# A six-layer decoder on one core: PSUM banks paired freely, the context transposed ahead of the kernel, and a new instruction order

## The chip, the cores and the metric

The kernel runs on one core of one Trainium2 chip. The metric is the device time of one execution in microseconds (us), as the median of several runs. TensorE is called PE, VectorE DVE, ScalarE ACT, GpSimd POOL and SyncE, which issues all transfers here, SP.

## The reference

Sixteen entries of 256 tokens by 256 features pass six layers, each followed by a residual sum and a layer norm without weights. `ctx_1024` is a second input of 16 x 256 x 256. Everything is float32.

```python
x = _layernorm(x + _L0_attn_ref(x, ...))                     # linear attention over 16 heads per token, then an MLP of 1024
x = _layernorm(x + _L0_xattn_ref(x, ctx_1024, ctx_1024, ...))  # 16 heads, softmax over keys at most 64 tokens away
x = _layernorm(x + _L0_ffn_ref(x, ...))                      # six cells, each 8-head softmax attention over three earlier nodes
x = _layernorm(x + _L1_attn_ref(x, ...))                     # causal linear attention, 16 heads
x = _layernorm(x + _L1_xattn_ref(x, ctx_1024, mask, ...))    # 16 heads, softmax over all 256 keys, mask on the keys
x = _layernorm(x + _L1_ffn_ref(x, ...))                      # fft, one matrix in the frequency domain, ifft: one 256 x 256 product
```

In both cross attentions the context goes through key and value projections: `k = key @ Wk.T + bk`, `v = value @ Wv.T + bv`.

## The kernel before, in words

**Data.** An entry is held as ten slots of 128 x 512 floats in `work` (four entries at a time, `NS = 4`), as tokens by features or, for a matmul's contraction, as features by tokens. Weights stay in `weights`, or pass through a ring of four slots that SP refills (`stream`). The eight PSUM banks (2 KB per partition each, 128 x 512 floats) are declared as four tensors `banks0` to `banks3` of two banks each.

**Order.** The program is a list of steps: `setup_steps` folds weights once, `entry_steps` names an entry's steps. A step has an engine, a name, a duration for the planner, the steps that it needs and the banks that it takes. `program_plan` walks through time with these durations, and whenever an engine is idle it starts the waiting step of the earliest entry, among them the one with the longest `tail` (the path behind it, times a drawn factor between 1 and 1.3). The result, `PLAN`, is for each engine a fixed list of steps; five functions (`tensor`, `vector`, `scalar`, `gpsimd`, `sync`) turn it into instructions and semaphore waits. So each engine runs its list in order, and a step that waits holds up all behind it on its engine.

**Banks.** `pick` chooses banks: a step of kind `score` or `kept` takes a whole tensor (banks 2u and 2u+1), a step of kind `misc` or `ctx` one bank, among banks 4 to 7 or beside one already taken. `take` makes PE wait for the eviction of what the bank held before. A semaphore `s_evicted` exists for each pair (0 to 3) and for each bank used alone (4 to 11, bank b is 4 + b).

**Softmax attention** (`heads`, 20 times per entry, four or eight heads' worth each): `s` multiplies queries by keys into two pairs (line L872), DVE takes the maxima of each pair (L1233), `nm` transposes them on PE into one bank (L883), ACT copies them (L1450), `st` multiplies again, transposed and less the maximum, into two pairs (L897 and L901; with L729 for the band mask), ACT takes the exponential of each pair into SBUF (L1466), `pv` multiplies by the values (L925, and L932 for the row sums in the cells) into the bank that `kept` left over.

**Other steps the text names.** `transposes` (L707) turns an entry's 256 x 256 block by four PE transposes into one bank, and ACT or DVE evicts it. `ctx_t` does so with the context when an entry is loaded (slot RAW into slot CT, for `x_k` and `x_v`), `ctx_t2` again before `y_k`, from a second load (`again`, L1727, into slot AGAIN), as CT is reused by the cells. `a_qkv` projects the first layer's queries, keys and values; its eviction (L1189) adds biases that lie in `row`, which SP loads in one transfer (L1706). `mix1` and `mix2` are that layer's products on POOL (L1614, L1624) and sums on DVE (L1199, L1203), 16 pieces per entry.

## Time and profile before

| | |
|---|---|
| median of 3 runs | 3605.32 us (3601.53 to 3610.42) |
| the profiled execution: its span (first to last instruction) | 3599.7 us |
| PE busy | 3245.1 us (90% of the span) |
| DVE busy | 2282.5 us (63%) |
| ACT busy | 1713.9 us (48%) |
| POOL busy | 1019.3 us (28%) |
| mean granted clock of PE | 0.974 |

The profiled execution was taken apart from the three timed runs, and only its span is known; the median lies 5.6 us above the span. Busy time is the time in which an engine had at least one instruction in work. Each float32 matmul of the code stands as two records in the profile, a transpose as one.

### The profile page before, as it was taken

The numbers are of one execution on the slowest core, as the hardware profiler recorded it, in microseconds if no ns is written. First come the engines' busy times: TensorE is split into PE (matmuls) and PEld (weight loads), VectorE is DVE, ScalarE is ACT, GpSimd is POOL, SyncE is SP. The second block draws the span as 40 slices with busy tenths as digits, with TensorE's granted clock in tenths as the row PEclk, the third lists the DMA queues.
The fourth block names the chain that finished last, engine by engine and source line by source line (L and its number), as shares of the span: only waits on it lengthen the run. The fifth ranks groups of instructions, "written<-read, shape, count | busy, mean of one in ns | idle before, by whom it ended". The sixth has DMA issues, their size and how long they took to land.

```text
span 3599.7 us, 77605 instructions
## 1 busy us (share of the span) xinstructions
PE 3245.1 (90%) x31500; PEld 2402.1 (67%) x31500; DVE 2282.5 (63%) x4093; ACT 1713.9 (48%) x3466; POOL 1019.3 (28%) x795
## 2 busy tenths in 40 slices
PE   7899989999989989999999999999999999998876
PEld 6777666666676667766666776666677666766654
DVE  6665757647766766667676666767667576465633
ACT  1245454544545454554545555454555545554532
POOL 7942305103242504214060421506042150000000
PEclk9899999999999999999999999999999999999987
DMA  6211010100011101011010101101010110000000
GB/s 213 71 45 39 22 42 16 31 31 22 23 51 31 36 13 49 25 35 35 17 45 16 48 25 31 36 19 45 16 48 25 31 35 15 31 16 13 13 7 4
DMA packets 123132, 122.88 MB, mean 34 GB/s; under 512 B 9760, under 2 KB 122656, under 8 KB 122656
## 3 DMA queue, kind: packets, MB, share of 16 engines
q1 hardware_dynamic: 122784, 117.91, 10.9%
q8 instruction: 258, 4.23, 0.5%
q14 instruction: 90, 0.74, 0.1%
HBM read 113.69 MB, written 4.19 MB: 33 GB/s over the span
## 4 chain that ended last, share of the span: by engine, by line
PE 61%; DVE 13%; POOL 9%; ACT 8%; issue 7%; DMA 1%; SPq 0%; DVEq 0%; POOLq 0%; ACTq 0%
PE banks L722 16%; PE banks L714 13%; PE banks L897 7%; PE banks L925 6%; PE banks L872 6%; DVE nmx L1233 5%; POOL work L1614 5%; ACT work L1466 4%; POOL work L1624 3%; PE banks L707 2%; PE banks L883 2%; PE banks L729 2%; PE banks L932 2%; PE banks L901 1%; PE banks L1004 1%
## 5 line engine op out<-in xcount | busy, mean ns | idle before, releaser
L722 PE MATMUL banks<-work,weights 128*128 128x256 f32 x3584 | 861.9, 388 | 40.5 <-DVE work L1256 22.1
L1233 DVE TENSOR_REDUCE nmx<-banks 128x4 f32<-128x1024 f32 (+1 forms) x640 | 720.9, 1165 | 251.5 <-PE banks L872 249.1
L722 PEld LDWEIGHTS banks<-work,weights 128*128 128x128 f32 x3584 | 671.3, 192 | 177.1 <-issue 55.2
L1466 ACT ACTIVATE work<-banks 128x1024 f32<-128x1024 f32 (+1 forms) x640 | 596.5, 980 | 268.7 <-PE banks L901 266.9
L714 PE MATMUL banks<-weights,work 128*128 128x256 f32 x2688 | 661.0, 392 | 44.0 <-ACT work L1466 16.6
L714 PEld LDWEIGHTS banks<-weights,work 128*128 128x128 f32 x2688 | 505.0, 195 | 147.3 <-issue 47.7
L1624 POOL TENSOR_TENSOR work<-work 128x512 f32<-128x512 f32 x256 | 405.5, 1609 | 212.3 <-DVE work L1203 115.7
L897 PE MATMUL banks<-work 32*128 32x256 f32 (+1 forms) x5120 | 396.2, 396 | 46.2 <-issue 15.6
L872 PE MATMUL banks<-work 32*128 32x256 f32 (+1 forms) x5120 | 355.0, 393 | 36.2 <-issue 11.0
L1250 DVE TENSOR_TENSOR added<-work 128x1024 f32<-128x1024 f32 x192 | 261.5, 1363 | 171.7 <-ACT work L1466 164.1
L925 PE MATMUL banks<-work 128*32 128x256 f32 (+3 forms) x5632 | 334.6, 359 | 23.7 <-ACT work L1466 23.6
L1614 POOL TENSOR_TENSOR work<-work 128x512 f32<-128x512 f32 x256 | 341.0, 1358 | 49.8 <-DVE work L1199 32.2
L1658 POOL TENSOR_TENSOR work<-work,row 128x512 f32<-128x512 f32 x64 | 88.8, 1387 | 882.1 <-PE banks L707 882.1
L897 PEld LDWEIGHTS banks<-work 32*128 32x128 f32 x5120 | 213.3, 189 | 165.8 <-issue 97.3
L872 PEld LDWEIGHTS banks<-work 32*128 32x128 f32 x5120 | 234.9, 187 | 128.9 <-issue 108.3
L1365 ACT ACTIVATE work<-banks,cb 128x256 f32<-128x256 f32 x384 | 161.4, 473 | 251.7 <-PE banks L722 251.6
L925 PEld LDWEIGHTS banks<-work 128*32 128x32 f32 x5632 | 156.6, 110 | 163.8 <-issue 102.4
L1203 DVE TENSOR_REDUCE work<-work 128x32 f32<-128x512 f32 x256 | 173.1, 679 | 90.8 <-POOL work L1624 90.6
L1199 DVE TENSOR_REDUCE work<-work 128x32 f32<-128x512 f32 x256 | 172.2, 680 | 75.2 <-POOL work L1614 75.0
L1450 ACT ACTIVATE work<-banks 128x256 f32<-128x256 f32 x320 | 118.7, 385 | 189.7 <-PE banks L883 189.1
L707 PE MATMUL banks<-ident,work 128*128 128x128 f32 x896 | 140.1, 286 | 68.8 <-DVE work L1181 28.3
L901 PE MATMUL banks<-work,ones_bf 3*128 3x256 bf16 (+1 forms) x2560 | 191.4, 272 | 0.0
(157 smaller groups left out, 3518.3 us busy)
## 6 DMA issues: line engine op xcount, KB each, us to landing
weights<-in_w_all SPq DMA_DIRECT2D x322, 256.0 KB, 2.7
work<-in_w_setup SPq DMA_DIRECT2D x41, 256.0 KB, 5.5
work<-in_ctx SPq DMA_DIRECT2D x32, 256.0 KB, 2.9
work<-in_x SPq DMA_DIRECT2D x16, 256.0 KB, 3.0
out<-work SPq DMA_DIRECT2D x16, 256.0 KB, 2.2
weights<-in_w_all SPq DMA_DIRECT2D x1, 3072.0 KB, 16.9
row<-in_rows SPq DMA_DIRECT2D x1, 1664.0 KB, 10.1
mrow<-in_mask SPq DMA_DIRECT2D x16, 32.0 KB, 3.1
```

What stands on the lines that cost most here:

```text
L707: ins = e.transpose(b[:, f * 256 + c * P:f * 256 + c * P + P], src[:, c, f * P:f * P + P], ident[:, :])
L714: ins = e.matmul(b[:, m * 256:m * 256 + 256], xin[:, k, m * P:m * P + P], wslot(w)[:, k, :], start=(k == 0 and (m == 0 or closed)) if star ...
L722: ins = e.matmul(b[:, m * 256:m * 256 + 256], wslot(w)[:, k, m * P:m * P + P], xin[:, k, :], start=(k == 0 and (m == 0 or closed)) if star ...
L872: ins = e.matmul(b[g // 2][:, g % 2, cc * 256:cc * 256 + kk.stop - kk.start], q[32 * g:32 * g + 32, f, cc * P:cc * P + P], k[32 * g:32 * g ...
L897: e.matmul(b[g // 2][:, g % 2, o], k[32 * g:32 * g + 32, f, kc * P:kc * P + P], q[32 * g:32 * g + 32, f, qq], start=(kind != "x"), stop=False,
L901: ins = e.matmul(b[g // 2][:, g % 2, o], ones_bf[32 * g:32 * g + 3, :], upper(stored_nmax(s, a))[32 * g:32 * g + 3, qq], start=False, stop ...
L925: ins = e.matmul(b[32 * g:32 * g + 32, lo:hi], left, right[:, kc * 256 + lo - qq.start:kc * 256 + hi - qq.start], start=(kc == 0), stop=(k ...
L1233: e.tensor_reduce(nmax(s, n)[:, 2 * p:2 * p + 2, :], b, AX, ALU.max, negate=True).then_inc(*freed("max", n, p, i))
L1250: e.tensor_tensor(added[:, half], pt(half, 0, 4)[:, :, 0:S], pt(half, 0, 4)[:, :, S:2 * S], ALU.add).then_inc(*tell(vec[s], "added", a, i))
L1466: e.activation(dst, src, ACT.Exp).then_inc(*freed("exp", n, p, i))
L1614: e.tensor_tensor(big1, q.unsqueeze(2).broadcast_to([P, PH, NH, DH]), k.unsqueeze(1).broadcast_to([P, PH, NH, DH]), ALU.mult).then_inc(*te ...
L1624: e.tensor_tensor(big2, mix.unsqueeze(2).broadcast_to([P, PH, DH, NH]), v.unsqueeze(1).broadcast_to([P, PH, DH, NH]), ALU.mult).then_inc(* ...
```

## The change: what it does

1. **Banks.** One tensor `banks` holds all eight. A `score` or `kept` step may take any two free banks; it prefers neighbours. If they are not neighbours, the eviction (the maxima on DVE, the exponentials on ACT) is two instructions of half the size. A single bank may be any free one. One semaphore per bank; a pair uses that of its first bank.
2. **Context.** The host passes `ctx_1024` with its last two axes exchanged. It is loaded straight into slot CT. The steps `ctx_t` and `ctx_t2` and their evictions are gone; `again` waits for `ck` of cell 5 (the last reader of CT's content) where it waited for `cv` of cell 5.
3. **Order.** `tail` is multiplied by ten drawn factors (one up to 1.3, nine up to 1.08, from other seeds). The planner adds 0.2 us (ACT) or 0.06 us (DVE) for a split eviction.
4. **Biases.** The first three rows of `row`, those of `a_qkv`, are loaded on their own, between entry 0's x and its context; the rest after entry 1's x.

```diff
-BANKS, PAIRS, HALVES, LONG = 8, 4, 2, 2
-SINGLE = range(4, BANKS)
+BANKS, HALVES, LONG = 8, 2, 2
...
-    ctx_t = through("ctx_t", 0, 0.44, "ACT", 0.49, load)
...
-            again = do("SP", "again", 0, 2.6, cv[c])
-            ctx_t2 = through("ctx_t2", 0, 0.44, "ACT", 0.48, again, ck[c])
-            y_k = through("y_k", 0, 1.75, "DVE", 0.66, ctx_t2, ("DVE", "centre", "y_k"))
+            again = do("SP", "again", 0, 2.6, ("PE", "ck", c))
+            y_k = through("y_k", 0, 1.75, "DVE", 0.66, again, ("DVE", "centre", "y_k"), also=(("PE", "co", c - 1),))
...
-    tail = [t * (1 + 0.3 * v) for t, v in zip(tail, rng.random(len(steps)))]
+    for n, seed in enumerate(SEEDS):
+        spread = 0.08 if n else 0.3
+        tail = [t * (1 + spread * v) for t, v in zip(tail, np.random.default_rng(seed).random(len(steps)))]
...
-                found = [u for u in range(PAIRS) if bank_left[2 * u] and bank_left[2 * u + 1]]
-                if found:
-                    bank_left[2 * found[0]] = bank_left[2 * found[0] + 1] = False
+                found = sorted(((u, v) for u in range(BANKS) for v in range(u + 1, BANKS) if bank_left[u] and bank_left[v]),
+                               key=lambda u: (u[1] - u[0] > 1, neighbours(bank_left, u[0]) + neighbours(bank_left, u[1]), u))
+                for u in found[:1]:
+                    bank_left[u[0]] = bank_left[u[1]] = False
...
-                found = sorted((u for u in range(BANKS) if bank_left[u] and (u in SINGLE or not bank_left[u ^ 1])), key=lambda u: (bank_left[u ^ 1], -u))
+                found = sorted((u for u in range(BANKS) if bank_left[u]), key=lambda u: (neighbours(bank_left, u), -u))
...
+                if apart(e, i, n):
+                    us += 0.2 if e == "ACT" else 0.06
...
-        pair = [ctx.enter_context(nc.psum_tensor(f"banks{u}", [P, 2, 512], F32)) for u in range(PAIRS)]
-        unit = pair + [pair[b // 2][:, b % 2, :] for b in range(BANKS)]
+        banks = ctx.enter_context(nc.psum_tensor("banks", [P, BANKS, 512], F32))
...
-        evicted = [signal(f"s_evicted{u}") for u in range(len(unit))]
+        evicted = [signal(f"s_evicted{u}") for u in range(BANKS)]
...
+        def spans(*key):
+
+            u = home.get(key, (0, 1))
+            if u[1] == u[0] + 1:
+                return [(0, 2, banks[:, u[0]:u[0] + 2, :])]
+            return [(j, j + 1, banks[:, u[j]:u[j] + 1, :]) for j in range(2)]
...
-                    once("rows")
-                    if a == 0:
-                        e.wait_ge(*when("ctx_t mm", i))
+                    once("first rows")
...
+                    for j, end, b in spans("max", n, p, i):
+                        ins = e.tensor_reduce(nmax(s, n)[:, 2 * p + j:2 * p + end, :],
+                                              b.rearrange("p j (c n) -> p j c n", c=NC)[:, :, :, 0:w], AX, ALU.max, negate=True)
+                    ins.then_inc(*freed("max", n, p, i))
...
+                    for j, end, b in spans("exp", n, p, i):
+                        dst = pt(half_of.get((i, n), 0), 2 * p + j, end - j).rearrange("p j (c n) -> p j c n", c=NC)[:, :, :, 0:w]
+                        ins = e.activation(dst, b.rearrange("p j (c n) -> p j c n", c=NC)[:, :, :, 0:w], ACT.Exp)
+                    ins.then_inc(*freed("exp", n, p, i))
...
-                    e.dma_start(slot(s, RAW), of_entry(ctx_in, i)).then_inc(*tell(in_ctx[s], "ctx", i))
+                    if i == 0:
+                        e.dma_start(row[:, 0:FIRST_ROWS, :].rearrange("p r n -> p (r n)"),
+                                    rows[0:FIRST_ROWS * D].partition_broadcast(P)).then_inc(*tell(in_first_rows, "first rows"))
...
+                    e.dma_start(slot(s, CT), of_entry(ctx_in, i)).then_inc(*tell(in_ctx[s], "ctx", i))
...
-                    e.wait_ge(*when("cv mm", 5, i))
-                    e.dma_start(slot(s, AGAIN), of_entry(ctx_in, i)).then_inc(*tell(in_ctx[s], "ctx again", i))
+                    e.wait_ge(*when("ck mm", 5, i))
+                    e.dma_start(slot(s, CT), of_entry(ctx_in, i)).then_inc(*tell(in_ctx[s], "ctx again", i))
...
-        "x": a["x"], "ctx": a["ctx_1024"], "mask": a["mask_BxS2_bk0"],
+        "x": a["x"], "ctx": a["ctx_1024"].transpose(0, 2, 1), "mask": a["mask_BxS2_bk0"],
```

The table of the order shows what this moves. The first place is the start of the program on PE. The names: `work` holds the entries' slots, `ident` is the identity, `s_loaded_ctx0` counts transfers of the context into entry slot 0, `s_vector0` steps of DVE on that slot (here layer norm 1). Before:

```order
L707 MATMUL banks3<-ident,work 128x128 [waits s_loaded_ctx0,s_setup_vector,s_setup_gpsimd]
L707 MATMUL banks3<-ident,work 128x128 x3
L707 MATMUL banks3<-ident,work 128x128 [waits s_evicted11,s_loaded_ctx1]
L707 MATMUL banks3<-ident,work 128x128 x3
L707 MATMUL banks3<-ident,work 128x128 [waits s_vector0]
L707 MATMUL banks3<-ident,work 128x128 x3
L714 MATMUL banks3<-weights,work 128x256 [waits s_evicted11,s_streamed_weights0,s_evicted10]
```

Now (L732 is the line of the transposes, L739 that of the projections):

```order
L732 MATMUL banks<-ident,work 128x128 [waits s_vector0,s_setup_vector,s_setup_gpsimd]
L732 MATMUL banks<-ident,work 128x128 x3
L739 MATMUL banks<-weights,work 128x256 [waits s_evicted7,s_streamed_weights0]
L739 MATMUL banks<-weights,work 128x256 x3
L732 MATMUL banks<-ident,work 128x128 [waits s_vector1]
```

The two groups of transposes of the context ahead of entry 0's first projection are gone. Over the whole program PE has 896 transposes on this line before and 768 now, ACT 112 copies of such blocks (128x512) before and 80 now.

The second place is the middle of the program on PE, where entry 7 (its maxima are in `nmx3`) goes through the last attention. `s_vector3` stands for DVE's maxima being ready; `s_evicted2` is the semaphore of pair 2, that is of `banks2`, and `s_evicted9` that of bank 5, its second half. Before:

```order
L901 MATMUL banks1<-work,ones_bf 128x256 x2
L901 MATMUL banks2<-work,ones_bf 128x256 x2
L883 MATMUL banks2<-ident,nmx3 128x128 [waits s_evicted2,s_vector3]
L883 MATMUL banks2<-ident,nmx3 128x128
L872 MATMUL banks0<-work 128x256 [waits s_evicted0,s_evicted3,s_evicted9]
L872 MATMUL banks0<-work 128x256
L872 MATMUL banks3<-work 128x256 x2
L872 MATMUL banks0<-work 128x256 x2
L872 MATMUL banks3<-work 128x256 x2
L883 MATMUL banks2<-ident,nmx3 128x128 [waits s_evicted9,s_vector3]
```

Now (L917 and L921 are the lines of `st`, L903 that of `nm`, L945 that of `pv`; `s_evicted0` is the semaphore of bank 0 and of the pair of banks 0 and 1):

```order
L917 MATMUL banks<-work 128x256 [waits s_evicted4,s_evicted1,s_evicted0]
L917 MATMUL banks<-work 128x256 x3
L921 MATMUL banks<-work,ones_bf 128x256 x4
L917 MATMUL banks<-work 128x256 x4
L921 MATMUL banks<-work,ones_bf 128x256 x4
L917 MATMUL banks<-work 128x256 [waits s_evicted7,s_evicted6,s_evicted2]
L917 MATMUL banks<-work 128x256 x3
L921 MATMUL banks<-work,ones_bf 128x256 x4
L917 MATMUL banks<-work 128x256 x4
L921 MATMUL banks<-work,ones_bf 128x256 x4
L903 MATMUL banks<-ident,nmx3 128x128 [waits s_evicted0,s_vector3]
```

Before, the transposes of the maxima take a bank of `banks2` straight behind the group that wrote `banks2`. Now a second whole `st` group stands between the group that wrote banks 0 and 1 and the transposes that take one of them.

Counted over the program, DVE takes 640 maxima of pairs before, and now 596 of pairs and 88 of single banks; ACT 640 exponentials of pairs before, and now 601 of pairs and 78 of single banks. So 44 pairs are split on DVE and 39 on ACT. PE changes between its three tile forms (full, 32 rows, 32 columns) 1453 times before and 1435 times now.

## Rows read from the trace of the kernel before

**Rows 1.** The page: busy time, share and instructions of each engine.

```profile
PE 3245.1 (90%) x31500; PEld 2402.1 (67%) x31500; DVE 2282.5 (63%) x4093; ACT 1713.9 (48%) x3466; POOL 1019.3 (28%) x795
```

**Rows 2.** Busy time of the engines in stretches (start, seven periods, end).

```profile
0.00:200.00 200.00, 163.75 (x968) 135.87 (x969) 133.05 (x259) 48.60 (x97) 166.67 (x148) 0.91 0.43 137
1395.70:1606.90 211.20, 196.37 (x1946) 145.19 (x1945) 140.66 (x253) 106.53 (x217) 63.96 (x48) 0.98 0.11 31
...
2660.75:2871.40 210.65, 195.45 (x1948) 144.62 (x1948) 141.44 (x253) 106.91 (x218) 63.32 (x48) 0.99 0.11 31
3400.00:3599.70 199.70, 137.49 (x1226) 95.98 (x1218) 78.81 (x152) 69.02 (x138) 6.48 (x7) 0.82 0.02 6
```

**Rows 3.** Timeline, SP: stores of entries 3, 12 and 15.

```profile
1145.36 0.38 SPq L1730 DMA_DIRECT2D out<-work  x1
...
3048.91 0.38 SPq L1730 DMA_DIRECT2D out<-work  x1
...
3597.03 0.38 SPq L1730 DMA_DIRECT2D out<-work  x1
```

**Rows 4.** Who PE waited for in 1806 to 2017 us (one period).

```profile
PE banks L722 <- DVE work L1256: 2.0, 1, 2.0
PE banks L925 <- ACT work L1466: 1.7, 2, 1.2
PE banks L897 <- issue: 1.6, 1, 1.6
...
PE banks L883 <- ACT work L1466: 1.2, 1, 1.2
```

**Rows 5.** Timeline, PE, 1963 to 1971 us.

```profile
1963.96 0.29 PE L901 MATMUL banks<-work,ones_bf 3*128 3x256 bf16 x4
1965.49 0.41 PE L883 MATMUL banks<-ident,nmx 128*128 128x128 f32 x2 [1.24 <-ACT work L1466]
...
1970.77 0.71 PE L897 MATMUL banks<-work 32*128 32x256 f32 x8 [0.73 <-ACT work L1466]
```

**Rows 6.** Timeline, ACT, same stretch.

```profile
1964.32 1.94 ACT L1466 ACTIVATE work<-banks 128x1024 f32<-128x1024 f32 x2 [1.50 <-PE banks L901]
```

**Rows 7.** Timeline, PE, 1861 to 1877 us.

```profile
1861.13 1.99 PE L722 MATMUL banks<-work,weights 128*128 128x256 f32 x8 [2.04 <-DVE work L1256]
...
1876.90 1.15 PE L897 MATMUL banks<-work 32*128 32x256 f32 x8 [1.60 <-issue]
```

**Rows 8.** Groups by line and shape (busy us, mean ns).

```profile
L1233 DVE TENSOR_REDUCE nmx<-banks 128x4 f32<-128x1024 f32 x512 | 603.8, 1218 | 232.6 <-PE banks L872 231.3
L1466 ACT ACTIVATE work<-banks 128x1024 f32<-128x1024 f32 x512 | 499.5, 1023 | 213.0 <-PE banks L901 212.5
L707 PE MATMUL banks<-ident,work 128*128 128x128 f32 x896 | 140.1, 286 | 68.8 <-DVE work L1181 28.3 <-DVE ykb L1089 10.2 <-ACT work L1466 7.4
L1203 DVE TENSOR_REDUCE work<-work 128x32 f32<-128x512 f32 x256 | 173.1, 679 | 90.8 <-POOL work L1624 90.6
L1310 DVE TENSOR_TENSOR work<-banks,causal 128x512 f32<-128x512 f32 x128 | 79.1, 680 | 13.2 <-PE banks L1004 13.1
L1393 ACT ACTIVATE work<-banks 128x512 f32<-128x512 f32 x112 | 66.1, 597 | 80.8 <-PE banks L707 80.6
```

**Rows 9.** Timeline of the start.

```profile
11.40 1.28 ACT L1393 ACT_TABLE_LOAD   x1 [11.40 <-PE banks L707]
...
13.68 0.56 SPq L1706 DMA_DIRECT2D row<-in_rows  x1
14.60 0.29 ACT L1371 ACTIVATE lnv<-mv,eps 128x2 f32<-128x2 f32 x1
...
18.18 3.78 PE L714 MATMUL banks<-weights,work 128*128 128x256 f32 x8 [1.11 <-ACT work L1365]
...
23.84 0.69 DVE L1189 TENSOR_TENSOR work<-banks,row 128x512 f32<-128x512 f32 x1 [4.52 <-issue]
```

**Rows 10.** Line L1727 (`again`): its transfers.

```profile
DMA to landing us min/median/max: 2.6/2.7/2.8
```

More of the change, by code:

```diff
@@ L200, in entry_steps @@
     x_t = through("x_t", 0, 0.44, "ACT", 0.48, x)
-    x_k = through("x_k", 0, 1.75, "ACT", 1.8, ctx_t, ("PE", "z2_t", 0))
+    x_k = through("x_k", 0, 1.75, "ACT", 1.8, ("PE", "z2_t", 0))
     x_v = through("x_v", 0, 1.75, "ACT", 0.56, clear)
@@ L340, in program_plan, with neighbours, apart @@
     bank, half, long_held = [True] * BANKS, [True] * HALVES, [0]
+    def neighbours(left, u):
+        return (u > 0 and left[u - 1]) + (u + 1 < BANKS and left[u + 1])
+    def apart(e, i, n):
+        return e != "PE" and any(j != "rest" and isinstance(held[i, m][j][1], tuple) and held[i, m][j][1][1] - held[i, m][j][1][0] > 1
+                                 for m, j in freed_by[n])
     def pick(takes):
@@ L794, in tensor @@
                     product(take("misc", "four", a), FOURIER[a][1]).then_inc(*tell(setup_pe, "four mm", a))
-                elif op == "ctx_t":
-                    e.wait_ge(*when("ctx", i))
-                    transposes(take("misc", "ctx_t", i), slot(s, RAW)).then_inc(*tell(pe[s], "ctx_t mm", i))
-                elif op == "ctx_t2":
-                    e.wait_ge(*when("ctx again", i))
-                    transposes(take("misc", "ctx_t2", i), slot(s, AGAIN)).then_inc(*tell(pe[s], "ctx_t2 mm", i))
                 elif op == "z_t":
@@ L1704, in sync @@
                         operand(f"{n}{a}", in_node[a], "node operands", a)
-                    if a == 2:
-                        e.dma_start(row[:, :, :].rearrange("p r n -> p (r n)"), rows.partition_broadcast(P)).then_inc(
-                            *tell(in_rows, "rows"))
                 elif op == "fourier":
```

96 lines of the change are left out of this document (48 added, 48 removed).

## The prediction

> **What bounds the kernel now.** I read the page's busy times first: PE works 3245 us of 3599.7, the next engine, DVE, 2283 [rows 1]. So PE is the bound, and 355 us are its idle time. The windows show where that lies [rows 2]: 36 us in the first 200, 62 in the last 200, and in between a repeating pattern. In seven periods, one for each entry, of 210.5 to 211.2 us, PE is busy 194.9 to 196.4 and idle about 15.3 (210.8 less 195.5), while DVE works 141 and ACT 106. The stores say how far the pattern carries: entry 3 is stored at 1145 us, entry 12 at 3049, nine periods of 211.5; the three entries behind it end at 3597 [rows 3]. A gain can come from less work on PE, or from smaller gaps in it.
>
> What the gaps are is in the waits of one period [rows 4]: one of 2.0 us behind DVE's weighing of a head pair (L1256), then many of 0.4 to 1.6 us behind the exponentials (L1466) and some that the profile puts down to nothing ("issue"). One of them can be read exactly. At 1965.49 us PE waits 1.24 us to transpose maxima [rows 5]. In the order of before, these transposes take a bank of `banks2` straight behind the `st` group that filled `banks2`, so they stand until both exponentials, 1.94 us from 1964.32, are done [rows 6]. PE's work was ready; a bank was not.
>
> **The change, part by part.** Against the profiled execution's 3599.7 us:
>
> *Transposes of the context.* PE loses 128 of 896 transposes. They take 140.1 us / 896 = 0.156 us each [rows 8], so 20 us. Bounds: 10, if half of them stood in gaps that stay; 30, with their share of the idle time before this line, 68.8 / 896 x 128 = 10. ACT loses 32 copies of 0.6 us [rows 8], nothing on a half-idle engine. Value: -20.
>
> *Gaps in the middle.* The new order decides here. For every bank that PE takes, and every result that it needs, I added the durations of the matmul groups between the group that the eviction follows and the one that waits, and compared that with what the evicting instructions take (1.22 us for a pair's maxima, 1.02 for its exponentials [rows 8], the rest from their own groups). Where the matmuls are the shorter, the difference is a shortage. This is an estimate: it knows no queueing on DVE and ACT. It gives 9.4 us of shortage per entry before, for entries 3 to 12, against 15.3 measured, and 7.6 of the 9.4 are banks. It finds the wait above as 1.2 us. In the new order it gives 3.6. The difference, 5.8 us, times 10 entries is 58; scaled by 15.3 / 9.4 it is 94; and if a third of the removed shortages come back as queueing, 40. I take 60, near the unscaled end, as the part that the count doesn't explain may stay. Value: -60.
>
> *The first three entries and the start.* The same count gives 16.9 us per entry before and 9.3 now, 23 in all. At the start itself, ACT loads a table for the context's copy (at 11.40), and then a second one, so that layer norm 1 goes on at 14.60 [rows 9]. Without the copy one load of 1.28 us and the copy are gone from this path, about 2 us. The first projection ends near 22 (18.18 + 3.78), and DVE evicts it only at 23.84, when the biases are there (issued at 13.68 [rows 9]): their own early transfer gives 1.9 us more. Up to 27 in all; but the first 200 us also hold 167 us of POOL work [rows 2], which nothing here shortens, so 4 is the lower bound. Value: -20.
>
> *The end.* The last three entries have 29.7 us of shortage each before and 28.9 now: no gain. PE's idle 62 us at the end are one entry's own chain. Value: 0.
>
> *Split evictions.* On DVE 44 pairs are two instructions. A half-size one is nearest to the 128x512 read of banks of 0.680 us, so a split costs 2 x 0.680 - 1.218 = 0.14 us, 6 us in all; on ACT 2 x 0.597 - 1.023 = 0.17, times 39 is 7 [rows 8]. DVE has 70 idle us in a period and ACT 104; PE waits for a split only where a bank is short. Between 0 and 13. Value: +3. If the cover is gone, it is the full 13.
>
> *The second load of the context* now lands where `y_k` reads it, with no transpose between. It takes 2.7 us to land [rows 10]; between `ck` of cell 5 and `y_k` the new order has two attention groups and a projection, 4.5 us of matmuls. It stays hidden, and the weight loads behind it on SP with it. Should it be late, PE loses at most the 2.7 us per entry, 43 us. `x_v` waits for the first load, which is there half an entry before. Value: 0.
>
> *PE's clock.* The granted clock is 0.98 to 0.99 in the periods [rows 2]: a stretch of each runs at 1.2 instead of 2.4 GHz. It follows the largest gaps: after waits of 2.04 and 1.60 us the group of eight at 1876.90 takes 1.15 us, where its like takes 0.71 [rows 5, 7]. A mean of 0.985 over 211 us is 6 us at the low level, so 3 us lost. The new order has no shortage above 1.0 us in a period. Between 0 and 3 us per period, 0 to 36 over twelve; as the clock may fall for other gaps too, I take 8. Value: -8.
>
> The Trainium skill has a rule on this (TensorE: Matmul & The Clock Gate, "A second HAM failure mode: psum-queue depth-cycling"): small idle times between groups that cycle through PSUM banks can make the clock swing between its two levels and cost throughput. By that rule the clock's whole loss belongs to the gaps that go, and the term would be 36; the row allows it and doesn't prove it, so 8 stands.
>
> Sum: 20 + 60 + 20 + 8 - 3 = 105, so a span of 3495. The median of before lies 5.6 us above the span of its profile, and 3605.3 - 105 = **3500 us**. With all low ends (10 + 40 + 4 + 0 - 13 = 41, 3564) and most of the high ends (30 + 94 + 27 + 0 = 151, 3454) its own range is 3454 to 3564.
>
> **The rivals.**
>
> *The clock recovers too (12%).* As forecast, but the clock term is its upper bound: 28 us more, 3472. For it: the low clock follows the largest gaps. Against it: the mean of 0.98 to 0.99 is already near 1.
>
> *Banks were not what PE waited for (13%).* The gaps move: where PE found no bank it now finds DVE or ACT still at other work, since each engine runs a fixed list. Then only transposes and the start count: 20 + 4 - 3 = 21, 3584. For it: the largest wait of a period (L1256) and 6 of the 15 us are not in my count. Against it: the wait at 1965.49 is a bank's, and DVE is 67% busy.
>
> *No change (5%).* The transposes filled gaps, and the ends set the time: 3595 to 3615. Against it: PE is 93% busy in a period.
>
> *Slower (8%).* One mechanism: the drawn priorities put `mix2` and `mix1` sums (L1203, L1199, 0.68 us each, 32 per entry [rows 8]) ahead of maxima that PE waits for. In the new order such a sum stands directly ahead of a head group's maxima 26 times in the whole program, before 17 times. Each costs PE at most 0.68 us; the forecast's 105 us are used up at 105 / 16 / 0.68 = 10 such late maxima per entry. With 20 per entry: 3500 + 16 x 20 x 0.68 = 3718; with 12, 3630. Against it: 26 is under 2 per entry.
>
> **Chances and range.** The forecast has 62%. Within 0.3% (11 us) a measurement of this kernel can't tell a change from none. Faster by more: 62 + 12 + 13 = 87%; same 5%; slower 8%. The range must leave out no more than 2 in 10. Without the second rival it would; with it, it goes to 3585. It starts at 3450, the forecast's high end, which holds the clock rival too.
>
> **What would show it.** Right: a period of about 203 us (211 less 1.3 for transposes, about 6 for gaps and up to 1 for the clock) with PE busy 194 and idle 9; entry 3 stored near 1115; waits behind L1466 and L1233 cut by half; the last entry's 62 us unchanged; DVE and ACT busy times within 2 us per period of before; no wait of `y_k` for the transfer. Wrong: a period whose idle stays near 15 with other names in the waits (the second rival), or one in which PE waits for maxima behind L1203 (the last). The most likely error is the size of the middle term, which rests on a count of distances, not on a measured wait.

## The result, and the profile after

The changed kernel takes 3567.21 us (median; 3565.31 to 3568.85) against 3603.64 of the kernel before on the same chip: ratio 0.9906, 95% interval 0.9892 to 0.9920. It is faster, by 36 us and not by 105; the forecast of 3500 us missed, though 3567 lies inside its range. The profiled execution has a span of 3566.3 us (before 3599.7) and a mean granted clock of 0.964 (before 0.974).

First the page's busy times, then the windows of the changed kernel: 200 us at either end and one of the periods between two stores.

```profile
PE 3242.3 (91%) x31372; PEld 2395.2 (67%) x31372; DVE 2329.9 (65%) x4137; ACT 1695.1 (48%) x3472; POOL 1019.1 (29%) x795
```

```profile
0.00:200.00 200.00, 166.49 (x936) 138.35 (x937) 128.04 (x247) 46.24 (x93) 164.27 (x146) 0.86 0.43 136
1323.90:1535.50 211.60, 195.70 (x1940) 143.82 (x1936) 145.64 (x255) 105.41 (x216) 63.02 (x47) 0.98 0.11 31
...
3366.30:3566.30 200.00, 138.39 (x1200) 97.02 (x1200) 78.70 (x152) 68.74 (x140) 5.78 (x7) 0.80 0.02 6
```

A period still takes 211.6 us, PE busy 195.7 and idle 15.9; before it was 210.7, 195.4 and 15.3 (means of seven periods from store 4 to store 11). Nothing was won in the middle [rows 2]. The stores (SP, timeline) of entries 3, 12 and 15 say where the 33 us of span came from.

```profile
1112.24 0.38 SPq L1750 DMA_DIRECT2D out<-work  x1
...
3016.84 0.38 SPq L1750 DMA_DIRECT2D out<-work  x1
...
3563.73 0.38 SPq L1750 DMA_DIRECT2D out<-work  x1
```

Against [rows 3], entry 3 is stored 33.2 us earlier; from there to entry 12 it is 1904.6 us (before 1903.5), and from there to the end 547 (548). All of the gain is made before entry 3 is stored.

PE's waits in one period (1747.1 to 1958.7), the answer to [rows 4]:

```profile
PE banks L747 <- DVE work L1275: 4.3, 1, 4.3
PE banks L892 <- DVE nmx L1251: 2.0, 3, 0.8
PE banks L903 <- DVE nmx L1260: 1.8, 1, 1.8
PE banks L892 <- issue: 1.6, 2, 1.3
...
PE banks L732 <- ACT work L1482: 0.4, 2, 0.2
```

The waits behind the exponentials (L1482, before L1466) are indeed nearly gone: over the whole run PE's fell from 88 to 23 us. Those behind the maxima were not cut by half, as the prediction had it, but rose from 59 to 72 (L1251, before L1233); those behind the last step of splitting the maxima rose from 16 to 36 (L1260, before L1241), behind the weighing from 33 to 55 (L1275, before L1256), behind the layer norms' last step from 28 to 48 (L1201, before L1181). The largest is one wait of 4.3 us at `co` (a cell's output projection) of cell 0 (L747), in every period. The timeline shows how it arises:

```profile
1857.55 7.08 POOL L1641 TENSOR_TENSOR work<-work 128x512 f32<-128x512 f32 x4
...
1859.79 0.61 PE L952 MATMUL banks<-added,ones 128*32 128x256 f32 x8
1860.10 0.69 DVE L1221 TENSOR_REDUCE work<-work 128x32 f32<-128x512 f32 x1 [0.23 <-POOL work L1641]
...
1862.32 2.59 DVE L1191 SCALAR_TENSOR_TENSOR work<-work,mv,row 128x256 f32<-128x256 f32 x2
...
1864.95 0.88 DVE L1197 SCALAR_TENSOR_TENSOR work<-work,rstd 128x256 f32<-128x256 f32 x2
1865.75 0.42 DVE L1275 TENSOR_TENSOR work<-banks,work 128x256 f32<-128x256 f32 x1
...
1866.31 3.75 PE L747 MATMUL banks<-work,weights 128*128 128x256 f32 x8 [4.29 <-DVE work L1275]
```

PE has the attention's values and their row sums ready at 1860.4. The weighing by these sums (L1275) stands on DVE behind a sum of the second mix of entry i+3, which waits for GpSimd, and behind layer norm 5 of the entry before, whose first step, two instructions (L1191), takes 2.59 us while GpSimd multiplies. ScalarE's inverse sums stand behind that layer norm's root in the same way. The eight matmuls behind the wait take 3.75 us, at a granted clock of 0.66 from 1866.3 to 1873.0; such a group takes 1.97 elsewhere.

### The profile page after: what moved, and what is told of

The parts are those of the page before. It is cut to its first block, busy times and chain, and to the rows that moved or that the text cites. A ratio compares the mean times of both kernels' runs of the same rounds, so it can differ in the third digit from the quotient of the medians.

```text
span 3566.3 us, 77500 instructions
## 1 busy us (share of the span) xinstructions
PE 3242.3 (91%) x31372; PEld 2395.2 (67%) x31372; DVE 2329.9 (65%) x4137; ACT 1695.1 (48%) x3472; POOL 1019.1 (29%) x795
## 4 chain that ended last, share of the span: by engine, by line
PE 60%; DVE 15%; ACT 9%; issue 8%; POOL 7%; DMA 1%; SPq 0%; DVEq 0%; POOLq 0%; ACTq 0%
PE banks L747 16%; PE banks L739 11%; PE banks L892 7%; PE banks L917 6%; DVE nmx L1251 5%; PE banks L945 5%; POOL work L1641 3%; ACT work L1482 3%; PE banks L732 2%; PE banks L754 2%; PE banks L855 2%; PE banks L903 2%; POOL work L1631 2%; PE banks L952 1%; PE banks L921 1%
## 5 line engine op out<-in xcount | busy, mean ns | idle before, releaser
L747 PE MATMUL banks<-work,weights 128*128 128x256 f32 x3584 | 868.3, 390 | 56.4 <-DVE work L1275 51.5
L1251 DVE TENSOR_REDUCE nmx<-banks 128x4 f32<-128x1024 f32 (+3 forms) x684 | 725.4, 1099 | 250.5 <-PE banks L892 248.7
L747 PEld LDWEIGHTS banks<-work,weights 128*128 128x128 f32 x3584 | 678.3, 194 | 189.0 <-DVE work L1275 53.9
L1482 ACT ACTIVATE work<-banks 128x1024 f32<-128x1024 f32 (+3 forms) x679 | 595.1, 937 | 288.7 <-PE banks L921 288.7
L739 PE MATMUL banks<-weights,work 128*128 128x256 f32 x2688 | 653.7, 389 | 20.7 <-ACT work L1482 4.4
L739 PEld LDWEIGHTS banks<-weights,work 128*128 128x128 f32 x2688 | 499.3, 193 | 124.9 <-issue 39.7
L1641 POOL TENSOR_TENSOR work<-work 128x512 f32<-128x512 f32 x256 | 407.3, 1615 | 366.4 <-DVE work L1221 216.9
L917 PE MATMUL banks<-work 32*128 32x256 f32 (+1 forms) x5120 | 391.4, 394 | 18.0 <-DVE nmx L1251 6.8
L1631 POOL TENSOR_TENSOR work<-work 128x512 f32<-128x512 f32 x256 | 346.6, 1375 | 148.7 <-DVE work L1217 134.7
L1269 DVE TENSOR_TENSOR added<-work 128x1024 f32<-128x1024 f32 x192 | 281.3, 1469 | 129.3 <-ACT work L1482 118.7
L945 PE MATMUL banks<-work 128*32 128x256 f32 (+3 forms) x5632 | 341.2, 364 | 5.3 <-ACT work L1482 4.6
L917 PEld LDWEIGHTS banks<-work 32*128 32x128 f32 x5120 | 214.0, 190 | 132.1 <-issue 81.2
L945 PEld LDWEIGHTS banks<-work 128*32 128x32 f32 x5632 | 158.3, 111 | 148.4 <-issue 82.4
L1221 DVE TENSOR_REDUCE work<-work 128x32 f32<-128x512 f32 x256 | 173.2, 678 | 86.2 <-POOL work L1641 85.7
L1466 ACT ACTIVATE work<-banks 128x256 f32<-128x256 f32 x320 | 119.2, 385 | 212.7 <-PE banks L903 212.3
L921 PE MATMUL banks<-work,ones_bf 3*128 3x256 bf16 (+1 forms) x2560 | 190.8, 272 | 0.0
L732 PE MATMUL banks<-ident,work 128*128 128x128 f32 x768 | 122.1, 285 | 67.0 <-DVE work L1201 47.6
```

Of the source, the lines that this page charges most:

```text
L732: ins = e.transpose(b[:, f * 256 + c * P:f * 256 + c * P + P], src[:, c, f * P:f * P + P], ident[:, :])
L739: ins = e.matmul(b[:, m * 256:m * 256 + 256], xin[:, k, m * P:m * P + P], wslot(w)[:, k, :], start=(k == 0 and (m == 0 or closed)) if star ...
L747: ins = e.matmul(b[:, m * 256:m * 256 + 256], wslot(w)[:, k, m * P:m * P + P], xin[:, k, :], start=(k == 0 and (m == 0 or closed)) if star ...
L917: e.matmul(b[g // 2][g % 2][:, o], k[32 * g:32 * g + 32, f, kc * P:kc * P + P], q[32 * g:32 * g + 32, f, qq], start=(kind != "x"), stop=False,
L921: ins = e.matmul(b[g // 2][g % 2][:, o], ones_bf[32 * g:32 * g + 3, :], upper(stored_nmax(s, a))[32 * g:32 * g + 3, qq], start=False, stop ...
L945: ins = e.matmul(b[32 * g:32 * g + 32, lo:hi], left, right[:, kc * 256 + lo - qq.start:kc * 256 + hi - qq.start], start=(kc == 0), stop=(k ...
```

## The experiments

Each is compared with the changed kernel's 3567, which ran in one group only, or with a sister run; the kernel before ran beside every group of them, at medians of 3600 to 3603 us. A difference of 5 us between runs of different groups can't be told from none. Two constructions serve several. To **move** a step, the finished list of an engine is edited. To **choose banks anew**, the lists are run through the planner's own event loop with their order held, so that only the bank rule decides. In the code below `...` stands for what is not shown, and the comments are added.

**1. The norm first.**

```diff
+for i in range(2, 13):
+    advance("ACT", (i + 1, "norm", 5), (i, "ln_r", 5))            # puts the first step ahead of the second
+    advance("DVE", (i + 1, "norm", 5), (i, "ln_n", 5))
```

> The changed kernel with one inversion undone in the two fixed lists: for entries 3 to 13, ScalarE does cell 0's inverse sums ahead of the earlier entry's layer-norm root 5, and VectorE weighs cell 0's heads ahead of the earlier entry's normalising 5. Theory (the list order gives the bank gain back at TensorE's co): the wait of 4.3 us for the weighing falls under 1 us in each of 11 periods, about -3.4 us each, and the low-clock stretch behind it (3.75 us for eight matmuls that take 1.97 at full clock, and some more after) goes too, about -3 us each: 3567 - 11 x 6.4 = 3497 us (3485 to 3515), period near 205. Rival 1 (the idle time only moves to the next late work on VectorE): 3557 to 3570. Rival 2 (the wait goes, the clock does not recover): 3567 - 11 x 3.4 = 3530 us.

Measured: 3561.0 us. Rival 1 holds. The wait fell from 4.3 to 0.7 as meant, but the period fell only from 211.6 to 210.7, its idle time stayed at 15.9, and the next group of PE waited. The profile names nobody for that wait; it ends 0.24 us after the first maximum behind the same layer norm (1869.19 and 0.93 us):

```profile
1865.11 1.97 PE L761 MATMUL banks<-work,weights 128*128 128x256 f32 x8 [0.73 <-DVE work L1289]
1870.36 0.81 PE L768 MATMUL banks<-band,ident_bf 128*128 128x384 bf16 x4 [3.29 <-issue]
```

**2 to 4. Order and bank rule apart.** The old lists without the context's transposes, with their own banks; the old order with banks chosen anew under the new rule; the new order with fixed pairs.

```diff
+for e in PLAN:                                 # old_order, on the lists of the planner before
+    PLAN[e] = [as_banks(e, *s) for s in PLAN[e] if s[1] not in ("ctx_t", "ctx_t2")]
...
+ORDER = {e: [s[:3] for s in PLAN[e] if s[1] != "stream"] for e in PLAN}
+PLAN, STREAM = replay(ORDER)                   # new_order_fixed; old_order_any also leaves out ctx_t, ctx_t2
```

> The changed kernel's code with the lists of the kernel before (its order, its banks, fixed pairs), only the four context transposes and their evictions taken out: context from the host, early first rows and a semaphore per bank, without the new rule and the new draws. Theory: the transposes' 18 to 20 us and the 3.5 us of the start, nothing else: 3604 - 23 = 3580 us (3574 to 3590). Rival (these two make the whole gain, the bank rule and draws nothing): 3564 to 3570 us. Second rival (the freed time on TensorE turns into waits behind VectorE): 3590 to 3604.

Measured: 3595.2 us (ratio 0.9982, 0.9966 to 0.9997). The second rival: PE has less to do in a period (195.4 to 195.0), but the period stays 210.7. Transposes taken away in the middle give nothing: from entry 3's store to entry 12's it is 1902.6 us (before 1903.5).

> The same old order on every engine, but each product's banks chosen anew under the rule that any two free banks serve: the bank rule alone, without new draws. Theory (TensorE's waits behind the exponentials are waits for banks, and the rule removes most of them when the order stays): 5 us less per period than in the run with the old banks, about -55 us: near 3525 us (3510 to 3545). Rival (with the list order kept, the next wait takes their place): within 10 us of the run with the old banks, 3570 to 3590.

Measured: 3598.4 us. The rival: the rule alone is worth nothing in the old order.

> The changed kernel's order on every engine, with the banks chosen again as fixed pairs: the order alone, without the rule. Theory (the rule is worth some 5 us a period in this order too): 3567 + 12 x 5 = 3627 us (3600 to 3650). Rival (the rule is worth nothing, as the kernel's unchanged period suggests): 3560 to 3580 us.

Measured: 3756.1 us, 189 more than with the rule, further than the theory said; the period is 225.3. The new order, which was drawn for the rule, needs it. So the rule is worth 0 in one order and 13.7 us a period in the other.

**5 to 8. What the second mix does.** Three of VectorE's sums put behind the layer norms; GpSimd's products cut to 64 of 512 columns from entry 4 on, in the changed kernel and in that before; VectorE's sums cut to 4 of 32 results. All but the first leave out part of the computation.

```diff
+    for piece in (4, 7, 2):                                   # mix_later, for i = 2 to 12
+        put_behind("DVE", (i + 3, "mix2", piece), (i, "ln_n", 6))
...
+hs, ds = (PH, DH) if i < NS else (1, 4)                       # pool_light, before_pool_light
-e.tensor_tensor(big2, mix..., v..., ALU.mult)...
+e.tensor_tensor(big2[:, 0:hs, 0:ds, :], mix..., v..., ALU.mult)...
...
-e.tensor_reduce(q, big2, AX, ALU.add)...
+e.tensor_reduce(q[:, 0:1, 0:4], big2[:, 0:1, 0:4, :], AX, ALU.add)... # sums_light
```

> The changed kernel with three of VectorE's sums for the second mix (pieces 2, 7 and 4 of entry i+3) put behind the node layer norms 5 and 6 of entry i, for i = 2 to 12; nothing else moves. The run with the norm first showed that the chain co 5, layer norm 5, layer norm 6, then TensorE's r_t holds the period: VectorE works without a pause from 1858.5 to 1875. Theory (that queue on VectorE is what binds): three sums of 0.67 us leave the chain and GpSimd's product 4 with its slowing of VectorE comes later, -3 us a period: 3567 - 11 x 3 = 3534 us (3520 to 3548). Rival (the idle time moves on to the next late chain, or the second mix of entry i+3 becomes late for its product a_o): 3560 to 3580 us.

Measured: 3593.3 us; slower than the rival allowed. Layer norm 5's four instructions now took 1.8 us (3.5 in the changed kernel) and the wait of `co` 1.2, but PE had three new waits further on, of 1.9 us for a maximum behind the moved sums and of 1.7 and 1.8 us; the period is 213.5.

> The changed kernel, but from entry 4 on GpSimd multiplies only 64 of the 512 columns of each product of the second mix, so that part of the computation is left out; VectorE's sums stay as they are. Theory (GpSimd's products slow VectorE where they run together, and the new order puts them beside the layer norm that holds the period): the scalar_tensor_tensor of layer norm 5 falls from a mean of 1067 ns to near 565, the add beside it from 1.9 to 1.2 us, -2 us a period: 3567 - 12 x 2 = 3543 us (3530 to 3555). Rival (those instructions are not on the path that sets the period): 3560 to 3570 us.

Measured: 3502.7 us, more than the theory: the period falls to 206.6.

> The changed kernel, but VectorE sums only 4 of each piece's 32 results in the second mix, so that part of the computation is left out; GpSimd's products stay. VectorE loses about 9 us of 145.6 a period. Theory (VectorE's queue around the node layer norms binds): three of these sums are in the chain, -2 to -4 us a period: 3567 - 13 x 2.8 = 3530 us (3515 to 3545). Rival (TensorE's own order and the other chains bind): 3558 to 3570 us.

Measured: 3561.6 us. The rival: 4.8 us less work on VectorE in a period (145.6 to 140.9) and a period of 211.6 as before. VectorE's load is not what binds. Why shorter sums ahead of layer norm 5 don't bring it forward can be read:

```profile
1846.42 10.00 POOL L1641 TENSOR_TENSOR work<-work 128x512 f32<-128x512 f32 x6
...
1853.66 3.04 DVE L1191 SCALAR_TENSOR_TENSOR work<-work,mv,row 128x256 f32<-128x256 f32 x2
```

The sum ahead of it is 0.5 us shorter, and its own first step 0.5 us longer than in the changed kernel. In both this step ends 0.28 us after GpSimd's run of six products: at 1856.70 after 1856.42 here, at 1864.91 after 1864.63 in the changed kernel, and in the run with the norm first at 1867.29 after 1867.00. So the end of GpSimd's run, and no order on VectorE ahead of it, sets when this layer norm is done.

> The kernel before with the same part of GpSimd's products left out from entry 4 on. Theory (it is the new order that laid the products beside the layer norm; in the old one it takes 565 ns an instruction): no change, 3604 us within 0.3% (3593 to 3615). Rival (GpSimd slows VectorE on the path in the old order as well): 3590 us or less, the same 2 us a period as in the changed kernel or more.

Measured: 3551.9 us. The rival: the products cost the old order too, 3.6 us a period against 5.0 in the new.

**9 to 12. Mix earlier; every pair split; each half of the change undone in the planner.**

```diff
+move("PE", (j, "a_qkv", 2), ahead_of=(k, "nm", 4))            # values_early; i, k, m, j = i to i+3
+move("DVE", (j, "a_qkv", 2), ahead_of=(m, "ln_n", 3))         # and products and sums behind it
-            if u[1] == u[0] + 1:                              # all_split
-                return [(0, 2, banks[:, u[0]:u[0] + 2, :])]
+                found = [(u, u + 1) for u in range(0, BANKS, 2) if ...]   # replan_fixed
+    tail = [t * (1 + 0.3 * v) for ...default_rng(720053)...]  # replan_one_draw
```

> The changed kernel's order with the second mix of entry i+3 moved about 25 us earlier for i = 2 to 12: its third projection (a_qkv 2) on TensorE and VectorE, GpSimd's products and VectorE's sums; banks chosen again under the same rule, all work kept. Leaving out most of GpSimd's products gave 5.0 us a period and took the wait of co from 4.3 to 0.5. Theory (what costs is where the products lie: beside the node layer norm that TensorE waits for; VectorE idles about 7 us between 1821 and 1834, where they would now lie): 3 to 4 us a period less, 3567 - 11 x 3.5 = 3528 us (3515 to 3545). Rival (the slowing goes with the products wherever they are, as the kernel before gained 3.6 us a period too without them): 3555 to 3585 us.

Measured: 3566.0 us, the rival. No product runs beside layer norm 5 any more (481 ns an instruction, 1067 in the changed kernel), and the period is 212.0. VectorE stood waiting for GpSimd 5.5 us between 1845 and 1859, `co` still waited 2.8, and GpSimd has as much of the chain of waits as in the changed kernel (below), 17.5 us a period.

> The changed kernel with every pair evicted in two instructions, adjacent or not: some 37 more each on VectorE and ScalarE a period, of 0.15 and 0.19 us more a pair by the durations of the split ones, 5.5 and 7 us of busy time. Theory (TensorE waits for these engines at about ten places a period, and each such wait grows by 0.15 to 0.4): +2 us a period, 3567 + 30 = 3597 us (3580 to 3620). Rival (both engines idle a third of the time and hide it): within 10 us of 3567.

Measured: 3612.8 us, within the theory's range: 3.5 us a period for 2.4 us more work on VectorE and 2.2 on ScalarE, though VectorE idles 31% of the time and ScalarE half. Of the 3.5 us PE's idle time has 1.2; its busy time, at a granted clock of 0.97 in place of 0.98, has 2.3.

> The changed kernel with one part undone in the planner: only fixed pairs serve, singles as in the kernel before; the ten draws stay, and the planner draws up its lists anew with them. Theory (time follows the order that comes out more than the rule; these draws were not made for this rule): slower than the kernel before, 3620 to 3700 us. Rival (the rule gives nothing at all, the draws everything): 3560 to 3575 us.

Measured: 3726.9 us.

> The changed kernel with the other part undone: any two free banks, but one draw with the old seed and spread in place of the ten. Theory (the same: an order that was not picked is slower, rule or not): 3600 to 3700 us. Rival (the rule's gain holds with whatever draw): 3540 to 3580 us.

Measured: 3608.1 us, its middle 212.3 us a period, as the theory had it; the run before, at 3726.9, is slower than its theory's range. In both an order that was not drawn up with its rule loses what the change gained. Each is one drawn order, so how large the loss is for others is not shown.

By then the waits that were shortened by moving steps had come back as others. The chain of waits of the kernel before, read for one period, gave the theory for the next runs. From 1806 to 1861 it does not touch PE at all (pieces under 0.1 us are left out here and in the next):

```profile
1809.44 3.03 ACT work L1425 x8
...
1817.65 7.05 POOL work L1614 x5
1824.72 0.70 DVE work L1199
1825.49 6.34 POOL work L1614 x5
...
1855.49 2.33 POOL work L1624 x2
1857.83 0.69 issue
1858.52 1.51 POOL work L1624
1860.09 0.57 issue
1860.66 0.43 DVE work L1256
1861.13 0.92 PE banks L722 x3
```

ScalarE's gelu, then the first mix of entry i+3 on GpSimd (L1614) and VectorE, from 1832 to 1846 VectorE's queue of sums, maxima and a layer norm, then the second mix (L1624) and the weighing that PE waits for at 1861 [rows 7]. The changed kernel's chain leaves PE twice, for about 20 us through the first mix (L1622, L1631) and for 19 through the second (L1641):

```profile
1778.73 2.95 POOL work L1622 x2
...
1782.62 4.33 POOL work L1631 x2
...
1790.50 0.66 PE banks L732 x4
```

```profile
1847.53 0.70 DVE work L1207
...
1848.37 3.13 POOL work L1641 x2
...
1854.60 2.29 POOL work L1641 x2
1856.88 0.67 issue
1857.55 2.52 POOL work L1641
...
1863.20 1.72 DVE work L1191
1864.95 0.88 DVE work L1197 x2
1865.83 0.34 DVE work L1275
```

Added up over three periods, GpSimd has 25 us of this chain in each period before and 17.5 after. If this chain sets the period, PE's bank waits beside it cost nothing.

**13 to 15. Both mixes' products left out, in three kernels.** A small rest stays (4 of 32 rows), and the second mix is whole for entries 0 to 3.

```diff
-e.tensor_tensor(big1, q..., k..., ALU.mult)
+e.tensor_tensor(big1[:, 0:1, 0:4, :], q[:, 0:1, :]..., k[:, 0:4, :]..., ALU.mult)
-e.tensor_reduce(mix, big1, AX, ALU.add)
+e.tensor_reduce(mix, big1[:, 0:1, 0:1, :].broadcast_to([P, PH, NH, DH]), AX, ALU.add)
```

> The run with the old order and old banks, with nearly all of GpSimd's products of both mixes left out (4 rows of 32 in each piece of the first, 4 of 32 in each of the second, VectorE's sums of the first read one row over and over), so that part of the computation is missing. The chain of waits of the kernel before runs for 70 us of each period through ScalarE's gelu, GpSimd's and VectorE's mix of entry i+3 and comes back to TensorE only at 1861. Theory (that chain sets the period, and TensorE's waits for banks beside it cost nothing): without it the period falls by 5 to 8 us, 3595 - 12 x 6 = 3523 us (3500 to 3545). Rival (the products only slow VectorE, and leaving out those of the second mix gave all there is, 3.6 us a period): 3540 to 3555 us.

Measured: 3523.7 us, as the theory had it; period 205.4. GpSimd has no part in the chain now.

> The same products left out, old order, but banks chosen anew under the rule that any two serve. With the products in place the rule was worth nothing in this order (3598 against 3595). Theory (the rule's gain was hidden beside the chain through the mixes): now it shows, 2 to 3 us a period less than with the old banks, -25 to -35 us. Rival (the rule is worth nothing in this order, whatever else binds, since what stood behind the exponentials waited for their data): within 8 us of the run with the old banks.

Measured: 3507.5 us, 16 us less, 15 of them between entry 3's store and entry 12's. Between the two: the rule shows, at about half of what the theory named.

> The changed kernel with the same products left out. With those of the second mix alone left out it took 3503 us. Theory (chain through the mixes): its first mix stands on the chain too (two products and two sums, 6 us), so the time falls further, to 3485 us (3470 to 3497), and ends 50 to 65 us under the run with the old order and the same products left out, 28 of them from the first three entries as now. Rival (the rule and the new order are worth nothing in the middle): within 35 us of that run, and no lower than 3500.

Measured: 3438.5 us, 85 us under the run with the old order and 69 under that with the new rule; more than the theory said. The windows of one period each, first the old order, then the new:

```profile
1944.30:2149.50 205.20, 192.13 (x1938) 142.23 (x1937) 136.03 (x254) 105.18 (x214) 29.98 (x47) 1.00 0.11 32
```

```profile
1882.50:2083.40 200.90, 191.84 (x1942) 141.93 (x1938) 137.96 (x255) 105.41 (x216) 28.28 (x47) 1.00 0.11 33
2083.40:2285.30 201.90, 193.09 (x1940) 142.36 (x1936) 137.98 (x255) 105.42 (x216) 28.30 (x47) 0.99 0.11 33
```

Idle of PE is 13.1 us in a period of the old order and 8.9 in the new (means of seven). From entry 3's store to entry 12's it is 1859.0 us and 1815.4: rule and order together are worth 44 us in the middle once the mixes' products are out of the way (15 the rule alone in the old order, 28 more with the new order), and with the products in place they cost 2 (1902.6 and 1904.6).

**16 to 18. Orders that keep all the work.**

```diff
+    for piece, last in ((6, "split"), (4, "split"), (7, (1, 0)), (2, (0, 1))):   # sums_behind_max
+        put_behind("DVE", (i + 3, "mix2", piece), (i + 2, "split", 0) if last == "split" else (i + 2, "s", last))
...
+    places = [(i, "norm", 13), (i, "norm", 12), (i, "y_k", 0), (i, "y_ks", 0), (i, "y_kn", 0), (k, "add", 4), (i, "split", 15),
+              (k, "norm", 4), (k, "split", 5), (i, "add", 14), (i, "norm", 14), (i, "ln_n", 6), (m, "s", (0, 1)), (m, "s", (1, 0)),
+              (m, "split", 0), (m, "split", 1)]                                  # values_spread
```

> The changed kernel with VectorE's sums 2, 7, 4 and 6 of the second mix of entry i+3 behind the maxima of entry i+2 that follow layer norm 6, for i = 2 to 12, each behind another maximum. In the trace of the run with the sums behind layer norm 6, layer norm 5 took 1.8 in place of 3.3 us and the wait of co fell to 1.2, but TensorE then waited 1.9 us for the maximum behind the sums, and 1.7 and 1.8 more after it. Theory (the place of these sums decides): these waits stay under 2 us in all and the period falls by 2 us, 3545 us (3530 to 3556). Rival (what is taken from one wait comes back at the next, since the chain goes on through the second mix): 3560 to 3600 us.

Measured: 3591.5 us. The rival: PE waited 1.7, 2.5 and 1.8 us further on.

> As the run with the second mix moved earlier, all work kept, but of its 16 sums on VectorE eight lie in the idle stretch up to the maxima of cell 5, three before the layer norm of entry i and five behind its layer norm 6, so that VectorE does not stand waiting for GpSimd (5.5 us between 1845 and 1859 in that run) and no product runs beside layer norm 5. Theory (a chain through the mixes and that layer norm holds the period): the wait of co falls under 1 us and the period by 3 us or more, 3567 - 11 x 3 = 3534 us (3515 to 3550). Rival (the wait comes back behind the maxima of the next entry, as with the other moved sums): 3558 to 3590 us.

Measured: **3522.0 us** (3519.2 to 3530.6), ratio 0.9775 (0.9759 to 0.9791), as the theory had it: faster than both kernels, by 80 and 45 us. Against the run with the second mix moved earlier only the places of VectorE's sums differ. GpSimd has 7 us of the chain in a period, and the wait of `co` is no longer among the largest:

```profile
1940.00:2147.40 207.40, 194.22 (x1944) 142.24 (x1936) 147.09 (x256) 105.55 (x216) 61.77 (x47) 0.99 0.11 32
```

```profile
PE banks L1064 <- DVE nmx L1423: 2.4, 4, 0.7
PE banks L1075 <- DVE nmx L1432: 1.8, 1, 1.8
```

> The same, and the cell's norm ahead of the layer norm on both engines, as in the first run. Theory (the chain through layer norm 5 and 6 to r_t has room once GpSimd is away from it, so a co that comes 1 to 2 us earlier now counts): 5 to 20 us below the run without it, 3520 us. Rival (the two are alternatives, what one gives the other has given already): within 5 us of it.

Measured: 3538.3 us, 16 more than without it. Neither: the norm ahead of the layer norm now costs. PE has a wait of 1.7 us that was not there; the profile names nobody for it. That the next maxima come later, as in the first run, is the likely reason and not shown.

## Why the prediction was wrong

**The step that failed is the middle term, -60.** "PE's work was ready; a bank was not" was right for the wait that I read, and the count of shortages was right on the exponentials: the waits behind them did go. It was wrong on the maxima, behind which PE waited longer than before. What it could not carry is the step from a shorter wait to a shorter period. The period was not set by PE's own row of groups but by a chain that leaves PE for about 55 of its 211 us, through the two mixes on GpSimd and VectorE. With it in place the middle gained nothing (1904.6 us after 1903.5); with the products left out of both kernels it gained 44 us. PE's idle time there is 8.9 us a period, where I had forecast 9, but that is luck: it starts from 13.1 and not from 15.3, so the change took away 4.2 us and not 6.3. I had read the waits by engine and line, which say how long PE stood still, and not the chain, which says whether that mattered. "PE is the bound" was the false sentence: of 211 us of the chain, the pieces on PE add up to 118. VectorE's work was taken for harmless too: it rose from 140.7 to 145.6 us a period, where the prediction allowed 2.

**The rival "banks were not what PE waited for"** has the right time (3584 is nearer to 3567 than 3500) and the right sign in the profile, "a period whose idle stays near 15 with other names in the waits". Its reason is half right: the gaps moved to VectorE's fixed list, but the banks had been waited for. Its time is near by luck: it took 20 us from the transposes and 4 from the start, where 33 came before entry 3's store.

**Transposes, -20.** Their time did go: 768 of 122.1 us against 896 of 140.1, 18 us less on PE (L732). Of it the run with only this change and the early rows gained 8 us in all. My lower bound of 10, "if half of them stood in gaps that stay", was too high.

**First three entries and start, -20.** With a quarter of the transposes, 25 was forecast and 33.2 measured. The first projection is evicted at 20.29 in place of 23.84, 3.6 of the 3.9 us that the prediction read from [rows 9]; with the old order the lead at entry 3's store is 5.7 us, so some 27 come with the new order and its banks.

**Clock, -8.** The sign was wrong. The mean granted clock fell from 0.974 to 0.964. Between levels of 1.2 and 2.4 GHz that is 2 x 0.036 x 3566 = 257 us at the low level against 2 x 0.026 x 3600 = 187, some 70 us more, which costs up to 35 us. By the windows about half of that lies between the stores of entries 3 and 12, up to 2 us a period, and the rest in the first and last 200 us. I said that the low clock follows the largest gaps, and that no shortage above 1 us was left; there was a gap of 4.3, and behind it the groups ran at half speed. [rows 7] already spoke against so simple a rule: behind the gap of 2.04 us eight matmuls took 1.99 us, the full-speed time. The Trainium skill's rule that I weighed (TensorE: Matmul & The Clock Gate, "A second HAM failure mode: psum-queue depth-cycling") would have the loss go with the small gaps behind banks. The trace neither bears it out nor refutes it: waits behind exponentials and maxima together went from 147 to 95 us and the clock fell, but the long gap is new beside them.

**Split evictions, +3.** Their price was right: 684 ns for a half-size maximum, 2 x 684 - 1218 = 150 ns, and 2 x 610 - 1026 = 194 ns on ScalarE. That they are nearly hidden was not: with every pair split the kernel loses 46 us. What the few pairs apart cost here no run shows.

**End and second load, 0.** Right: 547 us from entry 12's store against 548, and no wait of `y_k` for a transfer.

**Not settled:** why the new order gains 27 us in the first three entries; how much of what the products cost is GpSimd's own time and how much the time for which they hold up VectorE, as leaving them out takes away both; and whether the chain through the mixes is the only one near 211 us. In the last version the period is 207.4, still 5 us above the run without the products, and the chain spends 50 us of it on VectorE.

## What to carry to other kernels

A wait on the busiest engine is worth its length only where the chain of waits runs through it. Read that chain for one period of the steady state, first, and add up its shares by engine: if it leaves the busiest engine for tens of microseconds, what lies beside that stretch gains little, and what shortens the stretch counts. A piece of the chain that is held up by work beside it, as layer norm 5 is here, does not end earlier because something ahead of it got shorter. Where engines run fixed lists, a removed wait that comes back under another name in the next list entry is the sign of it; then leave out the suspected work as a test before tuning orders.

## What the runs showed of the hardware

GpSimd's products hold up VectorE's instructions with two inputs in SBUF, the memory that both read. It is plainest for a subtraction of 8 columns, the last step of splitting the maxima, which takes 176 ns at the median. Here it starts 0.03 us after a product and ends with it, 1.25 us later, and PE waits 1.8 us for it in every period:

```profile
1808.23 1.25 POOL L1631 TENSOR_TENSOR work<-work 128x512 f32<-128x512 f32 x1 [2.96 <-DVE work L1217]
1808.26 1.25 DVE L1260 TENSOR_TENSOR nmx<-nmx 128x8 f32<-128x8 f32 x1
```

This wait is still there in the fastest version with all work kept (1.8 us behind L1432). Layer norm 5's first instruction, with and without the second mix's products beside it (the changed kernel, then the new order with both mixes' products left out; busy us and mean ns):

```profile
L1191 DVE SCALAR_TENSOR_TENSOR work<-work,mv,row 128x256 f32<-128x256 f32 x32 | 32.9, 1067 | 2.1 <-ACT rstd L1393 1.8
```

```profile
L1191 DVE SCALAR_TENSOR_TENSOR work<-work,mv,row 128x256 f32<-128x256 f32 x32 | 15.1, 514 | 2.1 <-ACT rstd L1393 1.8
```

The adds of halves (L1269) take 1.22 us alone and 1.92 beside a product, while the sums with one operand (L1221) stay at 0.68 beside them. The Trainium skill says so (SBUF — State Buffer, "Who interferes with whom"): a VectorE instruction with two inputs in that memory contends with a GpSimd instruction that reads it, one with a single input does not, outside the modes that use two ports. To take the products away from layer norm 5 is not enough by itself: its instruction takes 481 or 482 ns in five runs with all work kept, and these take 3593, 3591, 3566, 3538 and 3522 us. Nor is VectorE's busy time the measure: in the fastest of them it is 147.1 us a period against 145.6 in the changed kernel.

The low clock does not follow the sum of idle time. The old order without products is idle 13.1 us a period at a granted clock of 0.99 to 1.00; the new order without them is idle 8.9 us at 0.98 to 1.00; the run with the rule and one draw is idle 16.8 us at 0.98 to 1.00; the changed kernel, idle 15.9 us with one gap of 4.3 us, has 0.98.
